# A graph network in one kernel: gathers before scatters with counts five groups behind, and four of 25 subtractions of six chunks on VectorE

## The reference

```
x_i, x_j = ssp(ssp(x) @ W_i.T + b_i), ssp(ssp(x) @ W_j.T + b_j)
m   = x_i + segment_sum(x_j[dst] * (edge_attr @ W_att.T), src)
m   = three residual blocks of two dense layers each, then ssp
x   = layernorm(x + gate * x + m @ W_v.T + b_v)
```

## Time and profile before

| what | us |
|---|---|
| median of 3 runs | 3559.18 (3556.36 to 3571.11) |
| profiled execution, its own time | 3564.24 |
| its span, first to last instruction | 3562.4 |
| PE busy | 3187.2 (89%) |
| DVE busy | 2896.8 (81%) |
| POOL busy | 2663.7 (75%) |
| ACT busy | 999.1 (28%) |
| mean granted clock of PE | 0.958 |

### The profile page before, as it was taken

How to read it: one execution, slowest core, us unless ns; L and a number is a source line. 1 busy time by engine, 2 the same in 40 slices (tenths; PEclk the granted TensorE clock), 3 DMA queues, 4 the chain that set the end, 5 groups by cost and what they waited for, 6 DMA issues and landing times.

```text
span 3562.4 us, 64347 instructions
## 1 busy us (share of the span) xinstructions
PE 3187.2 (89%) x20040; PEld 1823.5 (51%) x20040; DVE 2896.8 (81%) x8886; ACT 999.1 (28%) x1689; POOL 2663.7 (75%) x1764
## 2 busy tenths in 40 slices
PE   4899999999999999999999999976788888899996
PEld 3566666666666666666666666642222222322222
DVE  6688888888888888888888888868677775877886
ACT  3111111111111111111111111133455554233433
POOL 2288888888888888888888888861787888476874
PEclk7999999999999999999999999987899999999998
DMA  8633333333333333333333333315545452232320
GB/s 311 247 49 50 45 44 50 50 50 49 50 44 45 49 50 50 49 50 46 44 49 50 50 49 50 39 2 151 151 127 150 129 151 75 78 89 76 89 64 9
DMA packets 265753, 271.38 MB, mean 76 GB/s; under 512 B 145252, under 2 KB 224717, under 8 KB 265673
## 3 DMA queue, kind: packets, MB, share of 16 engines
q1 hardware_dynamic: 90905, 163.09, 15.3%
q0 software_dynamic: 131712, 19.76, 12.7%
q10 hardware_dynamic: 43056, 87.49, 8.0%
HBM read 189.11 MB, written 81.07 MB: 76 GB/s over the span
## 4 chain that ended last, share of the span: by engine, by line
POOL 47%; PE 19%; issue 17%; DVE 6%; DMA 5%; ACT 3%; SPq 3%; POOLq 1%; DVEq 0%
POOL edge_counts L486 27%; POOL nodes_and_gaps L477 14%; PE PS L1404 6%; PE PS L1427 6%; DMA edge_counts<-small 4%; POOL scores L541 4%; PE PS L1436 3%; SPq L366 2%; POOL counts_and_logs L524 1%; DVE scores L1142 1%; DVE PS L1153 1%; DVE counts_and_logs L1128 1%; PE PS L1416 1%; DMA edge_counts<-counts_and_logs 1%; ACT scores L729 1%
## 5 line engine op out<-in xcount | busy, mean ns | idle before, releaser
L1303 PE MATMUL PS<-scores 128*128 128x320 bf16 x11760 | 1707.2, 303 | 132.5 <-DVE scores L974 69.1
L1303 PEld LDWEIGHTS PS<-scores 128*128 128x128 bf16 x11760 | 1156.9, 99 | 664.4 <-DVE scores L974 160.5
L486 POOL DMA_INDIRECT edge_counts<-small x752 | 1211.6, 1611 | 282.0 <-issue 282.0
L541 POOL TENSOR_TENSOR scores<-scores,max_of_targets 125x896 f32<-125x896 f32 x335 | 701.5, 2140 | 191.4 <-ACT max_of_targets L724 142.0
L477 POOL DMA_INDIRECT nodes_and_gaps<-xj_rows,small x588 | 580.9, 988 | 242.4 <-issue 162.8
L974 DVE TENSOR_SCALAR scores<-scores,small 128x192 bf16<-128x192 bf16 x3136 | 748.2, 304 | 3.5
L889 DVE SCALAR_TENSOR_TENSOR scores<-scores,small,PS 128x512 bf16<-128x512 f32 x784 | 573.0, 731 | 0.0
L1142 DVE TENSOR_TENSOR scores<-PS,counts_and_logs 125x896 f32<-125x896 f32 x350 | 377.8, 1082 | 204.0 <-PE PS L1404 76.9
L624 ACT ACTIVATE scores<-nodes_and_gaps 128x512 bf16<-128x512 f32 x98 | 61.7, 630 | 1403.6 <-DVE nodes_and_gaps L952 929.8
L729 ACT ACTIVATE scores<-scores 125x896 f32<-125x896 f32 x350 | 329.9, 948 | 372.8 <-POOL scores L541 365.9
L1404 PE MATMUL PS<-q_features,k_features 64*125 64x448 f32 x1400 | 371.1, 612 | 68.0 <-DVE scores L1142 65.1
(11 more groups left out here) (192 smaller groups left out, 2124.0 us busy)
## 6 DMA issues: line engine op xcount, KB each, us to landing
counts_and_logs<-edge_counts SPq DMA_DIRECT2D x70, 980.0 KB
scores<-tile_keys ACTq DMA_DIRECT2D x96, 512.0 KB
edge_counts<-counts_and_logs SPq DMA_DIRECT2D x50, 766.0 KB
edge_counts<-counts_and_logs SPq DMA_DIRECT2D x35, 980.0 KB
running_max<-fetch_targets ACTq DMA_DIRECT2D x48, 312.5 KB
max_of_targets<-fetch_targets ACTq DMA_DIRECT2D x48, 312.5 KB
edge_counts<-small POOLq DMA_INDIRECT x752
nodes_and_gaps<-xj_rows,small POOLq DMA_INDIRECT x588
```

The lines of the kernel that those rows point to most:

```text
L486: pool.indirect_dma_start(cnt_dram, bass.IndirectOffsetOnAxis(ap=index[:, s:s + 1], axis=0), value[:, s:s + 1], None, compute_op=ALU.add). ...
L541: nc.gpsimd.tensor_tensor(t, t, MB, ALU.subtract).then_inc(sem("shifted"), 1)
L1303: ins = nc.tensor.matmul(PS[:, b, 0:HI * F], onehot[:, s, b * P:b * P + 128], spread[:, s, i].rearrange("p h f -> p (h f)"), start=first a ...
```

## The change

On POOL each group now begins with three gathers; the wait for staged counts and the four scatters come behind them, then three gathers and four scatters. The counts are those of the group five before (BEHIND = 5). The wait for the cleared table moves to the first scatter. As the loops run over pairs of groups, the first six groups (FRONT) stand ahead of the loop, the sixth with scatters. After the loop 40 scatters are left. The staging buffers of the counts are chosen by the parity of the group that is scattered. In attention, DVE does subtractions 8, 12, 18 and 22 of chunks 0 to 5, POOL the other 21.

```diff
+BY_VECTOR = (8, 12, 18, 22)
...
-BEHIND = 4
+BEHIND = 5
+FRONT = BEHIND + BEHIND % 2
...
         def by_vector(g, i):
 
-            return g == LAST and i % QN in (1, 3, 4)
+            return i % QN in (1, 3, 4) if g == LAST else g < CH - 1 and i in BY_VECTOR
...
             def scatter(h, s, index, value):
 
+                if isinstance(h, int) and h == s == 0:
+                    pool.wait_ge(sem("counts_cleared"), 16 * FILLS)
                 if s % ROUND == 0:
                     pool.wait_ge(sem("count_added"), 16 * G * h + 16 * s)
                     settled()
...
             def group(g, u, scatters):
                 pool.wait_ge(sem("targets_staged"), g + 1)
-                if scatters:
-                    pool.wait_ge(sem("counts_staged"), 2 * (g - BEHIND) + 2)
                 settled()
+                b = (u + BEHIND) % 2
                 for s in range(0, G, ROUND):
-                    if scatters:
-                        for e in range(ROUND):
-                            scatter(g - BEHIND, s + e, cidx[u], cnt[u])
                     for e in range(ROUND):
                         if s + e not in FETCHED:
                             gather(g, u, s + e)
+                    if scatters and s == 0:
+                        pool.wait_ge(sem("counts_staged"), 2 * (g - BEHIND) + 2)
+                        settled()
+                    if scatters:
+                        for e in range(ROUND):
+                            scatter(g - BEHIND, s + e, cidx[b], cnt[b])
 
             pool.wait_ge(sem("xj_stored"), 32)
             for g in range(BEHIND):
                 group(g, g % 2, False)
-            pool.wait_ge(sem("counts_cleared"), 16 * FILLS)
-            with pool.Fori(BEHIND // 2, NG // 2) as k:
+            for g in range(BEHIND, FRONT):
+                group(g, g % 2, True)
+            with pool.Fori(FRONT // 2, NG // 2) as k:
                 for u in range(2):
                     group(2 * k + u, u, True)
...
                 if counts is not None:
-                    stage_counts(g + 2 - BEHIND, u, counts)
+                    stage_counts(g + 2 - BEHIND, (u + BEHIND) % 2, counts)
...
-            for g in range(BEHIND):
+            for g in range(FRONT):
                 edge_group(g, g % 2, g // 2, g == 0, None if g < BEHIND - 2 else g == BEHIND - 2)
-            with dve.Fori(BEHIND // 2, NG // 2 - 1) as k:
+            with dve.Fori(FRONT // 2, NG // 2 - 1) as k:
                 for u in range(2):
                     edge_group(2 * k + u, u, k, counts=False)
```

## The result

The changed kernel took **3679.6 us** (median of 4 runs, 3672.3 to 3699.9) against 3560.3 for the kernel before (4 runs): ratio 1.034, 95% interval 1.029 to 1.039. That is 119 us slower, where 8 us faster was forecast, outside the range of 3508 to 3585. The profiled execution took 3699.9, its span is 3698.1: 135.7 us more than the span of before.

A forecast was written before the change was run, and what follows sets the result against it. It took POOL's unbroken rounds to pace the edge loop, and attention passes to keep PE, POOL and DVE busy. Part 1's -23 and part 2's +15 gave -8 us: 3551 from the median 3559.2, range 3508 to 3585.

The forecast's parts named there:

- the head start: Start of edge loop: nine more gathers fit into POOL's 53 us hole, so group 4 starts on DVE 20.7 us earlier.
- Part 1: Edge loop and tail: new order of POOL's gathers and scatters, forecast at -23 us (-29 to -17).
- The lock (b): Edge loop: messages stay locked to POOL's rounds of scatters and gathers; last message at 2304.7, 22 us earlier.
- mechanism (a): Edge loop: DVE, before staging counts, waits for the previous scatters; message 97 at about 2298, 28.5 us earlier.
- 3.06 us after its last start; the gathers between take 3.9: Edge loop on POOL: a scatter round's landing, which the next round awaits, is over before the gathers between end.
- 0, at most 4: Start of attention: charge in us for count loads coming late to ACT's first log after the scatter tail.
- Part 2: Attention: four of 25 subtractions moved to DVE in six passes, forecast at +15 us (-28 to +71).
- Shift i being done by DVE after score i, three tiles ahead of use: Attention passes: DVE's place for each moved subtraction; the walk summed four shifts to +2.1 us a pass.
- the shifts collide: Rival, attention: each shift meets a POOL instruction and costs DVE 2.96 us; +71 less 23, 3607 us; chance 0.12.
- POOL bounds the passes: Rival, attention: POOL's relief shortens each pass by 4 x 1.16 us; -51 in all, 3508 us; chance 0.14.
- Free pace: Rival: the edge loop's lock breaks (-28 us) and the attention shifts break even; 3531 us; chance 0.20.
- PE holes in each group behind DVE's wait: Sign in the edge loop that would show the forecast wrong; no size given.

The follow-up runs named there:

- part1_alone: Changed kernel with the old choice of subtractions, so only the new gather and scatter order: 3541.7 us on chip A, against 3564.5 for the kernel before.
- part1_four_buffers: Changed kernel with the old choice of subtractions, four staging buffers for counts instead of two and loops over four groups: 3576.1 us, against 3564.5 before.
- pool_later_late_stage: Changed kernel with the old subtractions, ten memsets on POOL ahead of the first scatter, counts staged behind DVE's third piece: 3553.9 us, against 3558.1 before.
- part1_third: The same kernel as part1_alone, measured a third time, on chip D: 3648.5 us, against 3558.1 for the kernel before.
- part2_only_12: Kernel before with subtraction 12 alone moved to DVE: 3577.5 us, against 3565.8 for the kernel before.
- part2_three_ahead: Kernel before with the four subtractions on DVE, each done three tiles earlier in DVE's order: 3562.2 us, against 3565.8 before.

## Why the prediction was wrong, point by point

**Held: the head start.** Message 4 unheld near 158 (155.3 to 160.1 in the profiles), the first scatter at 154 to 157 where no memset stands ahead of it, the first count loads on the edge: in part1_alone the last message stands at 2300.86 (2304 forecast), the last scatter ends at 2393.9 (2397), the first steepening at 2411.5 (2413). Part 1 was forecast at -23 and gave -23 on chip A. There the first log does wait for its load (3.01 us), as the charge of 0 to 4 allowed.

**Failed: "I take 23, bounds 21 and 29, because the lock has held for 93 groups".** The lock (b) was read rightly and taken for a property of the kernel. It is in the profile of before and in all eight on chips A and B (in part1_four_buffers 20 times), and in neither of the changed kernel's two, nor the other nine on chips C and D. Where it is missing, mechanism (a), DVE's wait for the scatters, sets the loop. The prediction put (a) at 2298 for the last message, with POOL's pace untouched; it stood at 2396.89 in the changed kernel, with a pace of 24.17 us a group. That was the mis-sized term.

**Failed: "3.06 us after its last start; the gathers between take 3.9".** One landing, read where no load was in flight, was taken for all. With (a) DVE keeps one fixed place in POOL's round, so ACT's loads meet the last scatter of each first round. The landing took 5.5 us, POOL waited 0.85 us a group more, the group grew by 1.1: 90 groups, some 100 us. The circle is closed: POOL waits for the landing, DVE for POOL, the loads for DVE. That the moved wait closes it, pool_later_late_stage shows; that the loads lengthen the landing is read from the traces, and no run took them away. Within one profile, though, their distance varies and the gap follows it. In the changed kernel the load of keys leaves 1.0 to 1.5 us ahead of the last scatter in 70 groups, and POOL's gap before the second round averages 0.94 us; in the 8 groups where it leaves up to 0.5 us ahead it is 1.82, in the 8 where it leaves up to 1 us behind 2.41. No loads are left to issue behind group 97, and there POOL does not wait, in any of the eight profiles with this pace (last scatter of the first round and first of the second, changed kernel):

```profile
2387.38 1.56 POOL L490 DMA_INDIRECT edge_counts<-small  x1 [0.30 <-issue]
...
2393.22 1.62 POOL L490 DMA_INDIRECT edge_counts<-small  x1 [0.30 <-issue]
```

**Too small: the tail.** The charge for late count loads was "0, at most 4". In part1_third ACT waits 8.92 us for the first of them, as the 40 scatters end 98.0 us after the last message (2398.66 to 2496.7); in part1_alone it was 93.0, as forecast, and the wait 3.01. DVE follows POOL there by 8 us instead of 15, so the net begins earlier against the scatters.

**Part 2, +15 forecast, +36 measured.** Two steps failed. "Shift i being done by DVE after score i, three tiles ahead of use" was taken for a margin; but ACT takes the exponentials in order, and what was three tiles ahead for score i + 3 left ACT and PE nothing, so that exponentials 8, 12 and 22 came 4 to 8.5 us late (part2_only_12: "cost about 1" was 3 a pass; part2_three_ahead: 0 for all four). And the walk took POOL's instructions as they stood before: relieved, POOL comes to its gap instructions at other times, and shift 22, charged 0.3, met one and took 4.95. The exclusion itself was right: subtraction 22 ends 0.96 us after POOL's instruction, 2746.29 against 2745.33. The rule that the Trainium skill gives (SBUF — State Buffer, SBUF: two separate sides), that whichever engine starts first keeps the shared ports for its whole instruction, agrees with this row too. The rival "the shifts collide", 3607 with part 1's gain, had a good part of the mechanism and was put at 0.12.

**The rivals.** "POOL bounds the passes" is dead: POOL gave up 4 us or more a pass in part2_three_ahead, and the pass went from 78.2 to 77.8. "Free pace" did come, on chips C and D, and turned into a wait instead of a gain. The list of what would prove the forecast wrong named "PE holes in each group behind DVE's wait"; the one rival with DVE's wait (a) let it eat the head start and no more (3574), and no rival let it slow POOL.

**Open.** Why PE's semaphore updates come late on chips A and B and not on C and D (last section). The chip of the first profiles is not known, and with four chips it can't be said that it is the chip and not something else that is fixed for a group of runs. No profile of the kernel before was taken on C or D; its pace is POOL's own there or here, since it took 3558 to 3566 on all four.

## What to carry to other kernels

A wait that is moved behind another engine's work may cost little by itself and still tie two engines into one phase; ask what else is issued at a fixed distance behind the waiting engine (here: loads), and what it meets in that phase. A wait for a landing must be sized at the landing under the worst traffic it can meet, not at the quiet one. Work given to a second engine has to be done well before the third engine's turn comes, in its order; the same four instructions cost 36 us late and nothing three tiles earlier.

## What the runs showed of the hardware

The same kernel (part 1 alone) took 3541.7, 3639.4 and 3648.5 us on three chips, each within 0.6% in its four runs, while the kernel before took 3558 to 3566 on all four. A comparison of two kernels on one chip would have given either sign for the same edit.

The traces differ with it, without an exception among the twenty profiles. Between 300 and 2200 us, on C and D and in the changed kernel's first profile, each of the some 940 to 990 recorded updates of PE's semaphores stands within 0.02 us of the end of a PE instruction. On A and B and in the profile of before, 174 to 274 of some 800 to 860 stand 0.7 us or more behind it, up to 4.1. In part1_alone these are 241, and every one comes 1.5 to 3.5 us after POOL started the first scatter of a round. So this is what ties DVE to POOL's rounds in the lock. The landings differ as well: a DMA of POOL's ends in 16 steps of its semaphore, 12544 for the 784 scatters. The profiles of C and D have 12515 to 12541 of them, those of A, B and before 4273 to 4769. What stands behind both is not shown.

DVE's waits add up accordingly. part1_alone has 157.6 us at L938 and none for scatters; part1_third has 74.5 and 162.9. So the late updates cost DVE about 1 us a group, and in the same runs it never came to the wait that cost POOL 1.1; that the one spares the other is read from the traces, as no run could switch the late updates off.
